# Scan preparation reordered: the second direction's projections between two halves of a convolution, e + 1 as a two-input operation, the sixth SiLU later

## The reference, cut to what matters

```python
x, z = jnp.split(xz, 2, axis=1)
x = silu(causal_conv1d(x, conv_w, conv_b))
x_dbl = jnp.einsum('rd,bdl->brl', x_proj_w, x)
dt_raw = x_dbl[:, :DT_RANK]
Bm = x_dbl[:, DT_RANK:DT_RANK + D_STATE]
Cm = x_dbl[:, DT_RANK + D_STATE:]
delta = jax.nn.softplus(jnp.einsum('dr,brl->bdl', dt_w, dt_raw) + dt_b[None, :, None])
# then h = h * exp(delta * A) + delta * u * B;  y = sum over states of h * C
```

## Time and profile before

| | us |
|---|---|
| median of 3 runs | 770.67 (770.21 to 775.93) |
| the profiled execution, whole | 771.34 |
| its span in the trace | 769.5 |
| busy in the span: DVE | 662.3 (86%) |
| PE | 634.9 (82%) |
| ACT | 503.2 (65%) |
| POOL | 454.2 (59%) |

### The profile page before, as it was taken

How to read it: one execution, slowest core, us unless ns; L and a number is a source line. 1 busy time by engine, 2 the same in 40 slices (tenths; PEclk the granted TensorE clock), 3 DMA queues, 4 the chain that set the end, 5 groups by cost and what they waited for, 6 DMA issues and landing times.

```text
span 769.5 us, 11619 instructions
## 1 busy us (share of the span) xinstructions
PE 634.9 (82%) x3947; PEld 374.1 (49%) x3947; DVE 662.3 (86%) x902; ACT 503.2 (65%) x598; POOL 454.2 (59%) x282
## 2 busy tenths in 40 slices
PE   7899999999997961577676777777877879899997
PEld 5655547678884420244453444445544554233332
DVE  7899996779975979999999998999999865788886
ACT  2657613779974768587886876778777710477673
POOL 3798883000001066799999998898999740533321
PEclk9999999999999995599998886889898899899999
DMA  2004100440001031000000000000000004100000
GB/s 56 5 13 103 26 1 12 79 97 7 3 3 59 14 78 41 1 0 1 1 0 1 0 1 1 0 1 0 1 2 0 1 4 96 42 1 0 14 1 14
DMA packets 28854, 14.98 MB, mean 19 GB/s; under 512 B 23023, under 2 KB 24943, under 8 KB 28655
## 3 DMA queue, kind: packets, MB, share of 16 engines
q1 hardware_dynamic: 27582, 13.61, 8.3%
q10 hardware_dynamic: 1216, 0.66, 0.4%
HBM read 5.14 MB, written 0.78 MB: 8 GB/s over the span
## 4 chain that ended last, share of the span: by engine, by line
PE 41%; DVE 25%; issue 5%; ACT 5%; POOL 5%; DVEq 0%; POOLq 0%; ACTq 0%
PE ps L572 37%; DVE arena L1379 14%; DVE ps L1055 6%; PE ps L754 4%; POOL arena L1780 3%; DVE arena L1055 2%; ACT arena L1733 1%; POOL x3t L1780 1%; DVE arena L1330 1%; ACT x L1733 1%; DVE arena L1332 1%; ACT arena L1619 0%; DVE arena L1268 0%; ACT x1t L1733 0%; ACT arena L1720 0%
## 5 line engine op out<-in xcount | busy, mean ns | idle before, releaser
L572 PE MATMUL ps<-arena 128*64 128x64 f32 (+5 forms) x2072 | 357.6, 357 | 106.6 <-DVE arena L1379 34.7
L572 PEld LDWEIGHTS ps<-arena 128*64 128x64 f32 (+5 forms) x2072 | 140.7, 138 | 238.7 <-issue 95.0
L1780 POOL TENSOR_TENSOR arena<-arena 128x1024 f32<-128x1024 f32 x81 | 188.3, 2336 | 25.0 <-DVE arena L1379 8.5
L1379 DVE TENSOR_TENSOR_SCAN arena<-arena,ps 128x1024 f32<-128x1024 f32 x66 | 150.9, 2287 | 9.0 <-DVE ps L1055 0.5
L1765 ACT ACTIVATE arena<-ps,nycol 128x1024 f32<-128x1024 f32 x64 | 71.1, 1114 | 55.3 <-PE ps L572 55.3
L1055 DVE TENSOR_TENSOR ps<-arena,ps 128x1024 f32<-128x1024 f32 x75 | 91.0, 1213 | 6.3 <-PE ps L572 5.6
L1720 ACT ACTIVATE arena<-arena,a_col 128x1024 f32<-128x1024 f32 x66 | 75.4, 1142 | 16.9 <-DVE arena L1379 16.4
L1900 POOL TENSOR_TENSOR arena<-arena,bmask 128x128 f32<-128x128 f32 x64 | 30.8, 482 | 76.4 <-PE ps L572 65.3
L1379 DVE TENSOR_TENSOR_SCAN arena<-ps,arena 128x1024 f32<-128x1024 f32 x30 | 68.2, 2273 | 3.9 <-POOL arena L1780 2.4
L1055 DVE TENSOR_TENSOR arena<-ps,arena 128x512 f32<-128x512 f32 (+2 forms) x71 | 48.4, 683 | 24.9 <-PE ps L572 18.5
L1619 ACT ACTIVATE arena<-arena 128x256 f32<-128x256 f32 x128 | 60.8, 503 | 11.7 <-DVE arena L1268 7.6
(11 more groups left out here) (208 smaller groups left out, 1049.9 us busy)
## 6 DMA issues: line engine op xcount, KB each, us to landing
arena<-arena SPq DMA_DIRECT2D x54, 64.0 KB
arena<-arena SPq DMA_DIRECT2D x12, 128.0 KB, 3.3
w_conv<-in_c_far SPq DMA_DIRECT2D x1, 1152.0 KB, 5.8
w_conv<-rpb_pad SPq DMA_DIRECT2D x36, 28.0 KB, 1.8
arena<-x SPq DMA_DIRECT2D x12, 64.0 KB, 2.0
arena<-x1t SPq DMA_DIRECT2D x12, 64.0 KB, 2.0
arena<-x3t SPq DMA_DIRECT2D x12, 64.0 KB, 2.0
arena<-arena SPq DMA_DIRECT2D x2, 288.8 KB, 3.7
```

Source lines behind the costliest of these rows:

```text
L572: return pe.matmul(o, l, r, start=start, stop=stop, **k)
L1379: ve.tensor_tensor_scan(hs_ring[n % RING], decay, add, 0.0, ALU.mult, ALU.add).then_inc(S("scan"), 1)
L1780: return gp.tensor_tensor(o, a, b, ALU.mult)
```

## The change

Five edits, all in the preparation of the scan.

1. PE: `conv_banks(5)` is cut in two. Its taps 0 and 1 stand where it stood; `bc_rows(1)`, `step_rows(2)` and `step_rows(3)` follow; then taps 2 and 3, and `bc_rows(2)` as before.
2. `w_diag` moves from a part of `delta[:, 3]`, which `relu_dt(3)` writes, to the second half of `x0`, since the taps are now read later.
3. DVE: e + 1 in `round_e` is a scalar_tensor_tensor, max(e + 1, e), in place of a tensor_scalar, for all six tiles.
4. DVE: for direction 0 both `relu_dt` come ahead of both `round_e`.
5. ACT: SiLU of tile 3 follows that of tile 2; SiLU of tile 5 moves behind `part_hi`, both `step_size`, both `exponential` and `part_mid` of direction 1. `part_mid` of directions 1 and 2 moves behind both `exponential` of its direction.

```diff
-        w_diag = delta[:, 3, 0:KC * P].rearrange("p (k n) -> p k n", k=KC)
+        w_diag = x0[:, HALF:T].rearrange("p (k n) -> p k n", k=KC)
...
-            def conv_banks(t):
+            def conv_banks(t, taps=range(KC)):
...
-                for k in range(KC):
+                for k in taps:
...
-                last.then_inc(S("conv_pe"), 1)
+                if k == KC - 1:
+                    last.then_inc(S("conv_pe"), 1)
...
             pe.wait_ge(S("x_sliced"), 2)
-            conv_banks(5)
+            conv_banks(5, range(0, KC // 2))
             pe.wait_ge(S("rest"), 1)
             bc_rows(1)
             pe.wait_ge(S("relu_dt"), 1)
             step_rows(2)
             pe.wait_ge(S("relu_dt"), 2)
             step_rows(3)
+            conv_banks(5, range(KC // 2, KC))
             pe.wait_ge(S("u"), u_count(5))
             bc_rows(2)
...
-                own(ve.tensor_scalar(one_e[t], du[:, t], 1.0, None, ALU.add))
+                own(ve.scalar_tensor_tensor(out=one_e[t], in0=du[:, t], scalar=1.0, in1=du[:, t],
+                                            op0=ALU.add, op1=ALU.max))
...
                 take_rest(dr)
+                if dr == 0:
+                    relu_dt(0)
+                    relu_dt(1)
+                    round_e(0)
+                    round_e(1)
+                    continue
                 for t in (PAIRS * dr, PAIRS * dr + 1):
...
-            activate(U_ORDER[3])
+            for t in U_ORDER[3:5]:
+                activate(t)
...
-            for t in U_ORDER[4:]:
-                activate(t)
             part_mid(0)
             for dr in (1, 2):
                 part_hi(dr)
                 step_size(2 * dr)
-                part_mid(dr)
                 exponential(2 * dr)
                 step_size(2 * dr + 1)
                 exponential(2 * dr + 1)
+                part_mid(dr)
+                if dr == 1:
+                    activate(U_ORDER[5])
```

## The result

| | before | changed |
|---|---|---|
| median of 20 runs each, us | 770.87 (767.46 to 776.09) | 775.25 (771.01 to 780.0) |
| ratio, with its 95% interval | | 1.0057 (1.0036 to 1.0078) |
| span of the profiled execution, us | 769.5 | 772.7 |
| DVE's last convolution ends, us | 265.2 | 263.0 |
| first scan starts, us | 309.11 | 310.47 |

The changed kernel is slower by 0.57%, 4.4 us (2.8 to 6.0). The stage that the prediction worked out, from the end of DVE's last convolution to the first scan, is 3.5 us longer in the two profiled executions. The point in the span at which it begins says nothing about the change: over all kernels of this study it lies between 262.9 and 267.2 us.

The account below looks back on a forecast made before the run. DVE's list was taken to bound the preparation: 4.2 us standing plus 3.3 longer e + 1 less 4.5 idle gives 3.0, the schedule 2.9, so the median 770.67 goes to 773.6 us; range 767.5 to 777.0.

Parts of the forecast that it names:

- What bounds the stage: DVE's operation list sets when the preparation ends; anything added to DVE's operations is paid in full.
- At most those 5.2 us by order: DVE's waits for ACT, all ahead of 291 us, are the most that reordering can give back.
- standing: Time SBUF-only rows of DVE take beyond their own length while held up by POOL; 7.2 us before, 11.4 forecast.
- The form stands behind POOL: The two-input e + 1 on DVE takes 1.23 us instead of 0.69 and still waits until POOL has finished.
- rival (a): DVE's e + 1 does not stand behind POOL, as both inputs are one tile: 2.9 us less, 767.8; chance 0.15.
- Who asked first goes first: When DVE and POOL operations on SBUF meet, the engine that asked first was taken to run first.
- The sum: In the preparation: 4.2 us lost to standing, 3.3 for the longer e + 1, 4.5 idle given back: 3.0 more.
- The clock: PE, idle 7.2 us, falls to 1.2 GHz; bc_rows(2) takes 3.9 instead of 1.94 us, then the clock comes back.
- Rival (b): PE's clock stays at 1.2 GHz through direction 2's projections: 5.0 us more, 775.7; chance 0.13.
- Rival (c): It cancels: the scan starts within 1 us of before, 770.7; chance 0.19.
- The new wait: Tile 1's round_e on DVE now meets POOL, standing 1.9 and 2.0 us; before, it was through ahead of POOL.
- the 12.4 us: DVE's idle and standing time in the preparation; 8 of it would have to go for a 1% gain, chance 0.02.

Follow-up runs that it names:

- late_part_lo: The changed kernel, but POOL waits for round_e of tiles 0 and 1 ahead of part_lo(0); stage 46.2 us, ratio to before 1.0029 (1.0001 to 1.0057).
- order_only: The changed kernel with e + 1 as the tensor_scalar again; stage 43.3 us, ratio to before 0.9987 (0.9958 to 1.0017).
- short_relu_less: The changed kernel with POOL's six relu_less cut to 8 of 1024 columns; stage 41.4 us, one run, 766.52 us.
- no_pe_gap: The changed kernel, but the second place of conv_banks(5) computes all four taps afresh; stage 47.0 us, ratio to before 1.0061 (1.0034 to 1.0088).

## Why the prediction was right, and where it was off

**What bounds the stage.** Right. DVE is idle for 0.9 us of 47.4, and everything that was added to it was paid. "At most those 5.2 us by order" left out that the order moves standing too: with POOL held back in late_part_lo it went from 11.9 to 11.2, and the stage down by 1.2.

**The form stands behind POOL.** Right, and rival (a) with it wrong: the row at 269.42 with the same tile on both inputs took 3.15 beside POOL. Alone it took 1.23 (267.02 and 290.07), the value chosen. The Trainium skill's page SBUF — State Buffer (Who interferes with whom) is the one of the two that this trace agrees with.

**Who asked first goes first.** Held at every meeting looked at: POOL at 268.96 ahead of DVE's 269.42, DVE ahead of POOL's next at 271.45. The forecast laid take_rest(1) 12.7 us behind the convolution; it came at 12.8. Tile 3 was to end at 24.1 and did at 24.3.

**The sum.** 3.0 by kinds (4.2 standing, 3.3 form, -4.5 idle) against 4.7, 3.3 and -4.3: every term has its sign, and the standing was 0.5 short. The schedule had part_lo(2) and tile 5 meet with 1.4 + 2.0 us of standing; it was 1.5 + 2.0. The rest is small change at each handover (in times_u 1.4 against 1.2) and an e4 that came 0.4 later.

**The clock.** The fall was right. It was to be back after some 4 us of work, and was after 4.4 us. Rival (b) did not come.

**Rival (c), it cancels.** Wrong for the change as a whole, but what the order alone does: 4.7 us of idle time against 4.4 of standing.

**The new wait.** "Before, this tile was through at 272.69 [...] that is the new wait" put too much on one meeting. With it taken out only 1.2 us came back.

**The time.** 2.9 us forecast, 4.4 measured with an interval from 2.8 to 6.0. So the medians lie just outside the "2 to 4 us more" that was given half the chance. Of this the stage is 3.5. The stated range, 767.5 to 777.0, also held (a) and (b), so it is the rows above that bear the forecast out, not that the median fell inside. In the sum for a gain of 1%, 7.7 us with 3.3 added, 11 and not 8 of the 12.4 us would have had to go.

The remaining 0.9 lies within the interval. Put in order, 13 of the 20 pairs of times lie 3.3 to 4.0 us apart, near the stage's 3.5; both medians lie at a jump in the order (3.8 below it, 5.0 above). The prediction's sign of being wrong, that the scans do not take the same 460 us to the end, came half: it is 460.4 against 462.2. But from the start of the first scan to that of the last it is 308.97 and 308.99 us, so the scans do carry the shift as it is. The 1.8 us come behind them, where no edit is, and 1.5 of them in three groups of PE in the last block, before and changed:

```profile
665.87 1.13 PE L572 MATMUL ps<-arena 128*128 128x512 f32 x2 [1.32 <-POOL arena L1900]
666.83 0.60 PE L572 MATMUL ps<-arena,w_attn 96*128 96x512 bf16 x2
667.26 1.02 PE L572 MATMUL ps<-arena 128*128 128x512 f32 x2
```

```profile
667.59 2.07 PE L572 MATMUL ps<-arena 128*128 128x512 f32 x2 [1.32 <-POOL arena L1910]
669.45 1.06 PE L572 MATMUL ps<-arena,w_attn 96*128 96x512 bf16 x2
670.31 1.19 PE L572 MATMUL ps<-arena 128*128 128x512 f32 x2
```

The granted clock was 1.00 from 665.1 to 669.1 before and 0.50 from 666.5 to 670.5 in the changed kernel. Over the ten kernels the way from the first scan to the end differs by up to 4 us (460.4 to 464.4). Whether the change has any effect there is open; the prediction gave it none.

## What to carry to other kernels

Where two engines share a port, add up the work of both on it and compare it with the stretch in which it runs. While that line is full, moving work earlier mostly turns idle time into standing (here 4.7 us into 4.4), and work taken off it shortens the stage only until the line has gaps and a wait for another engine takes its place. Rows that are longer than their own kind are the idle time that the idle column does not show; take the difference to the shortest of the kind before an order is changed. An operation moved off such a line should go where its new engine waits, and the waits behind it (here PE's idle time and its clock) have to be read again: six of them moved to ACT made the stage of before 0.7 us shorter, and two put into ACT's own idle time, with the clock mended, made that of order_only 2.4 shorter.

## What the runs showed of the hardware

An operation of 8 columns on POOL stood as long as a large one in the same place: in short_relu_less the first of the six took 1.18 us behind DVE's and the second 0.20 alone, so it stood 0.98, as the whole one did in the changed kernel (3.33 against 2.35).

```profile
271.31 1.18 POOL L1866 TENSOR_TENSOR arena<-arena 128x8 f32<-128x8 f32 x1
273.83 0.20 POOL L1866 TENSOR_TENSOR arena<-arena 128x8 f32<-128x8 f32 x1 [1.34 <-DVE arena L1335]
```

PE's clock can fall after work has begun again: in no_pe_gap PE resumed at 280.73 after 3.90 us idle, and the granted clock, 0.97 in the window from 280 to 282, was 0.50 in the next.

```profile
280.00:282.00 2.00, 1.27 (x6) 0.51 (x8) 2.00 (x1) 0.68 (x1) 1.59 (x1) 0.97 0.40 98
282.00:284.00 2.00, 2.00 (x5) 0.50 (x2) 2.00 (x3) 0.58 (x1) 1.19 (x1) 0.50 0.27 66
```
